# Cross-attention on one core: row sums in one block in a maximum buffer, a third score bank, a step's items in three places per tile, one bias transpose

## What is computed

```python
x = (hidden_states - mu) * jax.lax.rsqrt(var + LN_EPS) * ln_gamma + ln_beta
Q = _split_heads(x @ Wq.T)
K = _split_heads(memory_keys)
V = _split_heads(memory_values)
scores = jnp.einsum('bhsd,bhtd->bhst', Q, K) * scale
scores = jnp.where(mask, scores, -jnp.inf)
probs = jax.nn.softmax(scores, axis=-1)
attn = jnp.einsum('bhst,bhtd->bhsd', probs, V)
return residual + attn.transpose(0, 2, 1, 3).reshape(B, S, HIDDEN) @ Wout.T
```

## Time and profile before

| | us |
|---|---|
| median of 3 runs (734.58 to 739.43) | 737.66 |
| the profiled execution | 736.95 |
| its span, first to last instruction | 735.1 |
| TensorE matmuls busy | 692.0 (94%) |
| VectorE busy | 483.0 (66%) |
| GpSimd busy | 394.1 (54%) |
| ScalarE busy | 351.1 (48%) |

### The profile page before, as it was taken

The page is one execution under the profiler, slowest core; times in us unless marked ns, Lnnn a source line. Parts: engine busy times, 40 slices in busy tenths (PEclk is TensorE's granted clock), DMA queues, the critical chain, the costliest instruction groups (busy, mean ns, idle before and its releaser), DMA issues.

```text
span 735.1 us, 10854 instructions
## 1 busy us (share of the span) xinstructions
PE 692.0 (94%) x3585; PEld 397.1 (54%) x3585; DVE 483.0 (66%) x494; ACT 351.1 (48%) x614; POOL 394.1 (54%) x107
## 2 busy tenths in 40 slices
PE   2789999978999999999999999999999999999998
PEld 2578788534444444444444445444444444478886
DVE  6763432157688878878788887888878776653231
ACT  3741211434566666566666666666666656600000
POOL 1000000047296797967979679796797978930000
PEclk9799999979899999999999999999999999999999
DMA  9621100425426144161441614416244202213231
GB/s 339 180 65 36 44 14 1 119 50 128 100 61 158 38 123 110 51 157 37 122 109 50 157 40 120 111 48 157 49 109 94 84 14 88 86 66 122 98 114 57
DMA packets 39519, 68.10 MB, mean 93 GB/s; under 512 B 5285, under 2 KB 21799, under 8 KB 39471
## 3 DMA queue, kind: packets, MB, share of 16 engines
q1 hardware_dynamic: 39444, 67.64, 33.7%
q10 hardware_dynamic: 36, 0.01, 0.0%
HBM read 25.18 MB, written 4.19 MB: 40 GB/s over the span
## 4 chain that ended last, share of the span: by engine, by line
PE 84%; DVE 6%; SPq 4%; ACT 2%; DMA 2%; issue 2%; POOL 0%; ACTq 0%; DVEq 0%; POOLq 0%
PE SX L914 18%; PE MX L894 17%; PE PV L930 16%; PE MX L1058 12%; PE SM L920 6%; PE PV L857 5%; PE SM L857 4%; DVE mx L715 3%; PE MX L834 2%; SPq L303 1%; SPq L311 1%; DMA PR<-in_x 1%; PE SX L849 1%; PE MX L906 1%; PE MX L900 1%
## 5 line engine op out<-in xcount | busy, mean ns | idle before, releaser
L715 DVE TENSOR_REDUCE mx<-MX 128x1 f32<-128x1024 f32 x256 | 303.2, 1221 | 139.0 <-PE MX L894 138.7
L592 ACT ACTIVATE PR<-SX 128x512 f32<-128x512 f32 x512 | 277.4, 594 | 186.2 <-PE SX L914 186.0
L470 POOL TENSOR_TENSOR acc<-acc,PR 128x2048 f32<-128x2048 f32 x64 | 293.5, 4586 | 31.5 <-ACT PR L592 25.1
L470 POOL TENSOR_TENSOR acc<-PR 128x2048 f32<-128x2048 f32 x16 | 73.3, 4579 | 222.5 <-ACT PR L592 143.3
L914 PE MATMUL SX<-R 99*128 99x512 f32 x512 | 180.7, 432 | 3.2 <-ACT PR L592 2.9
L894 PE MATMUL MX<-R 97*128 97x512 f32 x512 | 165.0, 419 | 15.9 <-DVE mx L715 7.1
L914 PEld LDWEIGHTS SX<-R 99*128 99x128 f32 x512 | 88.7, 190 | 113.8 <-ACT PR L592 93.8
L894 PEld LDWEIGHTS MX<-R 97*128 97x128 f32 x512 | 89.6, 190 | 104.1 <-DVE mx L715 65.0
L930 PE MATMUL PV<-PR,C 128*32 128x512 f32 x1024 | 138.9, 615 | 0.1
L803 DVE TENSOR_TENSOR PR<-PR,MX 128x512 f32<-128x512 f32 x16 | 10.9, 687 | 53.3 <-PE MX L1058 51.8
L1058 PE MATMUL MX<-R 128*128 128x512 f32 x192 | 44.3, 390 | 0.0
(11 more groups left out here) (77 smaller groups left out, 520.3 us busy)
## 6 DMA issues: line engine op xcount, KB each, us to landing
R<-KTh SPq DMA_DIRECT2D x64, 256.0 KB, 4.3
PR<-in_x SPq DMA_DIRECT2D x16, 512.0 KB, 4.1
C<-in_ctx SPq DMA_DIRECT2D x16, 512.0 KB, 3.4
R<-KTl SPq DMA_DIRECT2D x64, 128.0 KB, 3.9
R<-QT SPq DMA_DIRECT2D x64, 128.0 KB, 2.5
acc<-in_L_xattn_Wq SPq DMA_DIRECT2D x8, 512.0 KB, 3.5
R<-QT SPq DMA_DIRECT2D x64, 64.0 KB, 2.1
C<-in_L_xattn_Wout SPq DMA_DIRECT2D x8, 512.0 KB, 3.3
```

What stands on the lines that cost most here:

```text
L470: nc.gpsimd.tensor_tensor(acc[:, :, :], a, PR[:, tt % RING, :, :], ALU.add).then_inc(pool_used, 1)
L592: nc.scalar.activation(PR[:, tt % RING, h, :], SX[h % 2][:, :], ACT.Exp, scale=SCALE).then_inc(exp_done, 1)
L715: nc.vector.tensor_reduce(mx[:, u % 2, c:c + 1], MX[par][:, :], mybir.AxisListType.X, ALU.max, negate=True).then_inc(mx_freed, 1)
```

## The change

- `row_sums`: the direct sums of two tiles and the sum of acc stand in one block of 24 matmuls, an item of slot 1 of the next step, and write into a maximum buffer MX instead of SM. GpSimd adds tiles 0 to 5; tiles 6 and 7 are the direct ones. VectorE turns the sums out of the MX buffer and frees it; the two other parts of the inversion follow the items of slots 2 and 3. After the last step the block stands behind the first two output projections and writes into SX[0].
- SM's bank becomes a third score bank: the scores of a step take the three banks in turn.
- Every slot has three places for items: ahead of the values, behind them, and behind scores 2 and 3; the schedules are written anew.
- The maxima lie in a row (column h * 4 + query tile), the bias is turned by one transpose, and BTh and BTl are 16 x 128 instead of 4 x 512.
- VectorE takes the keys' low part ahead of the query split, and SyncE stacks keys ahead of queries.
- The output projection swaps its two buffers.

```diff
-POOL_TILES = (0, 1, 2, 4, 5, 6)
+BANKS = 3
+PROBS = TT * HPG
+POOL_TILES = (0, 1, 2, 3, 4, 5)
+DIRECT_TILES = (6, 7)
 ADDS = len(POOL_TILES) - 1
-SUM_SLOT = 1
-FIRST_DIRECT = min(set(range(TT)) - set(POOL_TILES))
-SUMS_AT = (2, 5, 7)
-LAST_SUMS_AT = (2, 3, 4)
+SUMS_AT = (2, 3)
...
+def sums(a):
+    return [("sums", a, 0)]
...
 FIRST_STEP = [
-    ([], []),
-    ([], maxima(1, 0, 1)),
-    (maxima(1, 2), maxima(1, 3, 4)),
-    (maxima(1, 5), keys(2) + maxima(1, 6)),
-    (maxima(1, 7), maxima(1, 8, 9)),
-    (maxima(1, 10), maxima(1, 11, 12)),
-    (maxima(1, 13), maxima(1, 14, 15)),
-    (maxima(2, 0), bias(1) + maxima(2, 1, 2, 3)),
+    ([], [], []),
+    ([], maxima(1, 0), maxima(1, 1)),
+    (maxima(1, 2), maxima(1, 3), keys(2)),
+    (maxima(1, 4), maxima(1, 5), maxima(1, 6)),
+    (maxima(1, 7), maxima(1, 8), maxima(1, 9)),
+    (maxima(1, 10), maxima(1, 11), maxima(1, 12)),
+    (maxima(1, 13), maxima(1, 14), maxima(1, 15)),
+    ([], bias(1) + maxima(2, 0), maxima(2, 1, 2, 3)),
 ]
 STEP = [
-    ([], keys(2)),
-    (maxima(1, 4), maxima(1, 5, 6)),
-    ([], maxima(1, 7, 8)),
-    ([], maxima(1, 9, 10)),
-    (maxima(1, 11), maxima(1, 12, 13)),
-    ([], maxima(1, 14, 15)),
-    ([], maxima(2, 0) + bias(1)),
-    (maxima(2, 1), maxima(2, 2, 3)),
+    ([], maxima(1, 4), keys(2)),
+    ([], sums(-1), maxima(1, 5)),
+    ([], maxima(1, 6), maxima(1, 7)),
+    (maxima(1, 8), maxima(1, 9), maxima(1, 10)),
+    ([], maxima(1, 11), maxima(1, 12)),
+    (maxima(1, 13), maxima(1, 14), maxima(1, 15)),
+    ([], bias(1) + maxima(2, 0), maxima(2, 1)),
+    ([], maxima(2, 2), maxima(2, 3)),
 ]
...
     if n == STEPS - 2:
-        items[TT - 1] = (wout(0), wout(1))
+        items[TT - 1] = ([], wout(0), wout(1))
     if n == STEPS - 1:
-        items = [([], []) for _ in range(TT)]
+        items = [([], [], []) for _ in range(TT)]
         for o, tt in zip(range(2, WOUT_BLOCKS), (1, 2, 3, 5, 6, 7)):
-            items[tt] = ([], wout(o))
+            items[tt] = ([], sums(-1) if tt == 1 else [], wout(o))
...
-    BTh = sb("BTh", [HPG, S], F32R)
-    BTl = sb("BTl", [HPG, S], F32R)
-    mx = sb("mx", [P, 2, (ST - 1) * HPG + P], F32)
+    BTh = sb("BTh", [M_ITEMS, P], F32R)
+    BTl = sb("BTl", [M_ITEMS, P], F32R)
+    mx = sb("mx", [P, 2, P], F32)
...
-    SX = [nc.alloc_psum_tensor(f"SX{i}", [P, S], F32) for i in range(2)]
+    SX = [nc.alloc_psum_tensor(f"SX{i}", [P, S], F32) for i in range(BANKS)]
     PV = nc.alloc_psum_tensor("PV", [P, S], F32)
-    SM = nc.alloc_psum_tensor("SM", [P, S], F32)
-    QP = [PV, SM]
+    QP = [PV, SX[2]]
...
-                queries_split(n)
                 keys_split(n)
                 key_rows(u % RING)
+                queries_split(n)
                 query_rows(u % RING)
...
-                nc.scalar.activation(BTh[:, :], MX[par][0:HPG, 0:S], ACT.Copy).then_inc(bt_hi, 1)
+                nc.scalar.activation(BTh[:, :], MX[par][0:M_ITEMS, 0:P], ACT.Copy).then_inc(bt_hi, 1)
...
-            def exps(n, u, tt, pair):
-                    nc.scalar.activation(PR[:, tt % RING, h, :], SX[h % 2][:, :], ACT.Exp, scale=SCALE).then_inc(exp_done, 1)
-            act.sem_inc(exp_done, 2)
+            def exp(n, tt, h):
+                nc.scalar.activation(PR[:, tt % RING, h, :], SX[(HPG * tt + h) % BANKS][:, :], ACT.Exp, scale=SCALE).then_inc(exp_done, 1)
...
-                nc.vector.tensor_reduce(mx[:, u % 2, c:c + 1], MX[par][:, :], mybir.AxisListType.X, ALU.max,
+                nc.vector.tensor_reduce(mx[:, u % 2, i:i + 1], MX[par][:, :], mybir.AxisListType.X, ALU.max,
...
-                    nc.vector.transpose(rsum[:, :], SM[:, :]).then_inc(sums_turned, 1)
+                    nc.vector.transpose(rsum[:, :], bank).then_inc(sums_turned, 1)
...
                         if kind == "keys":
-                            if a == 2:
-                                split_queries(n + a)
                             key_low(n + a, at % 2)
+                            split_queries(n + a)
+                        if kind == "sums":
+                            invert_sums(n + a, 0, MX[at % 2][:, 0:S])
+                            dve.wait_ge(sums_turned, n + a + 1)
+                            dve.sem_inc(mx_freed, 1)
                         at += 1
+                    if tt in SUMS_AT and not first:
+                        invert_sums(n - 1, 1 + SUMS_AT.index(tt))
...
-            step(n, n % RING, items_of(n), LAST_PARITY, LAST_SUMS_AT)
+            step(n, n % RING, items_of(n), LAST_PARITY)
...
             for part in range(3):
-                invert_sums(STEPS - 1, part)
+                invert_sums(STEPS - 1, part, SX[0][:, :])
...
             def bias_item(n, u, par):
-                for st in range(ST):
-                    ins = nc.tensor.transpose(MX[par][:, st * P:(st + 1) * P], mx[:, u % 2, st * HPG:st * HPG + P], ident[:, :])
-                ins.then_inc(bt_ready, 1)
+                nc.tensor.transpose(MX[par][:, 0:P], mx[:, u % 2, :], ident[:, :]).then_inc(bt_ready, 1)
...
+            def score(n, u, tt, h):
+                at = HPG * tt + h
+                if at == 0:
                     pe.wait_ge(bias_in, 32 * (n + 1))
-                pe.wait_ge(exp_done, q + 1)
-                nc.tensor.matmul(SX[h % 2][:, :], KS[u % RING][0:ROWS, h, tt * P:(tt + 1) * P], QS[u % RING][0:ROWS, h, :],
+                if at >= BANKS:
+                    pe.wait_ge(exp_done, PROBS * n + at - BANKS + 1)
+                elif not is_first(n):
+                    pe.wait_ge(exp_done, PROBS * n - PROBS + max(b for b in range(PROBS) if b % BANKS == at) + 1)
+                elif SX[at] is QP[1]:
+                    pe.wait_ge(q_copied, 2 + BATCH * GROUPS)
+                nc.tensor.matmul(SX[at % BANKS][:, :], KS[u % RING][0:ROWS, h, tt * P:(tt + 1) * P], QS[u % RING][0:ROWS, h, :],
                                  start=True, stop=True).then_inc(scores_ready, 1)
...
-            def direct_sum(n, tt):
-                if tt not in POOL_TILES:
-                    if tt == FIRST_DIRECT:
-                        if not is_first(n):
-                            pe.wait_ge(sums_turned, n)
-                        ins = sum_probs(lambda h: PR[:, tt % RING, h, :], True, False)
-                    else:
-                        ins = sum_probs(lambda h: PR[:, tt % RING, h, :], False, False)
-                    ins.then_inc(tile_used, 1)
-            def last_sum(n):
+            def row_sums(n, bank):
+                for tt in DIRECT_TILES:
+                    sum_probs(bank, lambda h: PR[:, tt % RING, h, :], tt == DIRECT_TILES[0], False).then_inc(tile_used, 1)
                 pe.wait_ge(pool_used, ADDS * n + 2 * ADDS)
-                sum_probs(lambda h: acc[:, h, :], False, True).then_inc(sums_done, 1)
+                sum_probs(bank, lambda h: acc[:, h, :], False, True).then_inc(sums_done, 1)
...
+                for tt, (early, with_01, with_23) in enumerate(items):
+                    score(n, u, tt, 0)
+                    score(n, u, tt, 1)
+                    for item in early:
+                        mx_item(*item)
                     if tt >= 1:
                         values(n, u, tt - 1)
                     elif not first:
                         values(n - 1, u + RING - 1, TT - 1)
                     for item in with_01:
                         mx_item(*item)
-                    scores(n, u, tt, 2)
-                    scores(n, u, tt, 3)
-                    for item in with_23[:1]:
-                        mx_item(*item)
-                    if tt >= 1:
-                        direct_sum(n, tt - 1)
-                    elif not first:
-                        direct_sum(n - 1, TT - 1)
-                    if tt == SUM_SLOT and not first:
-                        last_sum(n - 1)
-                    for item in with_23[1:]:
+                    score(n, u, tt, 2)
+                    score(n, u, tt, 3)
+                    for item in with_23:
                         mx_item(*item)
...
             step(n, n % RING, items_of(n), LAST_PARITY, None, VECTOR_FREED_LAST)
             values(n, n % RING, TT - 1)
-            direct_sum(n, TT - 1)
...
-                        ins = nc.tensor.matmul(MX[q][:, cs], a[q][:, g, :], w[half][:, g, :],
+                        ins = nc.tensor.matmul(MX[1 - q][:, cs], a[q][:, g, :], w[half][:, g, :],
...
             project_out(0, 1)
-            last_sum(STEPS - 1)
+            row_sums(STEPS - 1, SX[0][:, :])
             pe.wait_ge(al_done, 2)
```

More of the change, by code:

```diff
@@ L113, in items_of @@
 def items_of(n):
-    items = [([i for i in with_01 if n + i[1] < STEPS], [i for i in with_23 if n + i[1] < STEPS])
-             for with_01, with_23 in (FIRST_STEP if n == 0 else STEP)]
+    items = [tuple([i for i in part if n + i[1] < STEPS] for part in slot) for slot in (FIRST_STEP if n == 0 else STEP)]
     if n == STEPS - 2:
-        items[TT - 1] = (wout(0), wout(1))
+        items[TT - 1] = ([], wout(0), wout(1))
     if n == STEPS - 1:
```

(65 more changed lines are left out.)

72 lines of the change are left out of this document (34 added, 38 removed).

## The result

The changed kernel takes 726.47 us (median, 725.48 to 727.08) against 737.83 of before: ratio 0.9848, 95% interval 0.9824 to 0.9871. A second measurement beside its variants gave 726.18 against 736.3, ratio 0.9866 (0.9843 to 0.9888). The forecast was 729 (722 to 738). The profiled execution has a span of 724.9 us, 10.2 less than before.

What follows compares the result with a forecast made beforehand. TensorE's own list of instructions was taken to set the time. Gains of 10.0 (steps 1 to 13), 0.6, 0.3 and 0.25 made 11.15, less 2.4 in step 0: 737.66 - 8.75 = 729 us, range 722 to 738.

Steps and rivals of the forecast that it cites:

- The price list of TensorE: TensorE's costs start to start, by neighbour: matmul pair 0.45, 32-column block 1.00, its turns 0.23, block before another block 0.88.
- rival without collision: Step 0: the query subtraction does not meet GpSimd's add, so 2.0 us is gained there: 724.5 us, chance 0.2.
- 721.5: Time if, besides no lock in step 0, the earlier low-clock stretch (6.8 us at half clock, worth up to 3.3) goes.
- the border stall: Slot 0 of each step: score 1 needs the last exponential's bank, so values stall 0.54 us.
- three blocks at 1.23 become 2.76, 1.05 gained: Row sums, slot 1: one merged block costs 2.76 instead of 3.69, values ahead 0.12 less; 1.05 us a step gained.
- the collision in step 0: Step 0: VectorE's query subtraction waits for GpSimd's third add, ending at 18.35 instead of 13.9; next step 2.4 us later.
- The thin slots: Most slots, one item behind scores 2 and 3 where two stood: TensorE stalls 0.12 us in an ordinary slot.
- The rival that ate the gain: Loop slots: the chain from scores to values is 0.1 longer in each, losing 11 us: 737 to 738, chance 0.2.
- The port lock: VectorE two-input operations and GpSimd operations exclude each other for a whole instruction; none expected in the loop, one in step 0.
- the chain of 1.58: In a slot, values may start 1.58 us after scores 2 and 3 are issued: 0.43 + 1.09 + 0.06.
- its sums move behind the first output projection, which saves their turns: Step 15: moved row sums save turns; with ScalarE's 0.4 longer delay set against it, 0.3 us gained.
- The term for `first_attn_high`: Step 15: ScalarE's `first_attn_high` stands about 0.4 us longer in the way.

Runs made afterwards that it cites:

- the bank experiment: The changed kernel, with the sequence of score banks skipping one bank once in a step, at score 2 of slot 1: 722.83 us, ratio 0.9817 against before.
- the experiment without the collision: The changed kernel, with VectorE splitting the queries of step 2 ahead of step 0's first maximum: 716.37 us, ratio 0.9739 against before.
- the parted sums: The changed kernel, with the sum of acc parted from the two direct sums by scores 2 and 3 in slot 1: 731.29 us, ratio 0.9925 against before.
- queries ahead of keys: The changed kernel, with VectorE splitting queries ahead of the keys' low part from step 1 on: 726.7 us, ratio 0.9868 against before.

## Why the prediction was right, and where it was off

**The price list of TensorE** carried the forecast. The merged sums came out at 2.69 for 2.76, the values ahead at 0.88 for 0.88, slot 2 at 3.14 for 3.15, slots 3 and 5 (348.70 to 352.41, 355.55 to 359.25) at 3.71 and 3.70 for 3.62, slot 6 at 3.39 for 3.37. The step was to be 29.55 and is 29.31. Two more terms held: GpSimd's fifth add was over 3.9 into the next step (365.88 to 369.75) for a forecast of 4.1, and the bias transpose took the 0.20 that was assumed (331.62 to 331.82).

The number alone would not have told this forecast from its rival without collision (724.5): 726.47 lies between the two. The subtraction of 4.87 in step 0 does. (That rival's second figure, 721.5, should read 721.2: 724.5 less 3.3.)

**The 0.24 a step.** Slot 0 was put at 4.09 and takes 3.73. Two terms were too large. The keys' transposes were taken at 0.97, the distance to a 32-column block in the earlier trace rows; in front of scores they take 340.31 - 339.52 = 0.79. And the border stall: values behind the first score at 0.91 instead of 1.10. The border costs more than this stall all the same: the first score waits there too, and the bank experiment won 0.44 a step.

**The merge by itself.** The term "three blocks at 1.23 become 2.76, 1.05 gained" is right for TensorE's list in the new order and wrong as a gain of its own: alone it made the kernel before slower by 1.9%, about a third of that by the collision in step 0. A kernel with merged sums and respread items but two banks is slower than before as well, by 3.7%: taking the third bank out of the new schedule costs 37 us. The working summed the whole step, which is why the total held.

**The thin slots.** One item behind scores 2 and 3 was to stall TensorE by 0.12 where it has nothing else. Scores to values are 0.64 for an unstalled 0.56: 0.08. The rival that ate the gain by 0.1 more a slot did not come.

**The port lock.** Foreseen by place and time: in the loop none (0.69 and 0.43 for the two operations), in step 0 a subtraction of 4.87 (counted from the first maximum: 13.2 to 18.35 forecast, 13.5 to 18.4 measured). Step 1 began 3.5 later than before, where 2.4 less 0.25 was forecast. Counted from the first maximum it was 38.5 for a forecast of 36.9, and the half clock behind the idle stretch, which the text named but took as even, is worth 2.0 of it. The price of the lost subtraction, 4.4, measured 4.2. The working took this 4.4 for the price of the whole collision. The cast's wait (2.1) and the clock (2.0) belong to it, and so the gain of the case without collision was put too low: the experiment reached 716.4 where that rival had 724.5 or 721.5. Behind this stands the Trainium skill ("SBUF — State Buffer", on the engine side): whichever operation starts first holds the shared pair for the whole instruction. The trace agrees: the third add's exponentials ended at 163.90, the subtraction could start at 164.44, and it ended behind the add.

**Step 1.** The half-clock stretch of the earlier trace rows is not in the changed kernel: its clock there is 1.00. From its first score to the next bias transpose step 1 took 28.09 before, and a later step 25.62 (340.96 to 366.58); the 2.5 between them fit the low clock (0.51 up to 191.40), and are more than half of the 4.11 in the table's second row. The text took this stretch and the new one in step 0 as even, and in size they were (2.5 and 2.0). But the one did not go because the other came: in the experiment without the collision the clock is 1.00 in both places. What went with the new schedule are TensorE's waits at the end of step 0 (from 178.5 to 185.9 it was busy 4.96 us of 7.40 before). The low-clock stretch in the rival "721.5" was thus not tied to the collision.

**The ends.** In step 14 (the table's fourth row) 0.05 was gained for 0.6. The keys' place is empty there, so scores follow scores with no item between, and the values start 1.57 behind the first of them (574.08 to 575.65). This is the chain of 1.58 that the working had priced, where TensorE's own list takes 1.01. Before, the missing keys made the step 1.4 shorter than the others; now it is 0.45 shorter.

The last part lost 2.8 where 0.3 was to be gained. Failed was "its sums move behind the first output projection, which saves their turns". The block there costs 645.29 - 642.58 = 2.71 where the sum of acc took 0.99, so 1.7 is lost behind the projection. Ahead of it one row-sum block less is left, but scores stand right behind scores in three places, and values start 1.65 to 1.76 behind them (595.69 to 597.34, 602.26 to 604.02, 616.61 to 618.29).

The term for `first_attn_high`, "about 0.4 longer", was right. TensorE waits for ScalarE, which waits for GpSimd's normalisation, in both kernels, and 0.34 longer in the changed one (before, then after):

```profile
633.47 0.99 PE L914 MATMUL SX<-R 99*128 99x512 f32 x2 [1.34 <-ACT PR L592]
```

```profile
621.46 0.78 PE L934 MATMUL SX<-R 99*128 99x512 f32 x1 [1.68 <-ACT PR L606]
```

Behind that wait the clock was low in the changed kernel's trace, where before it stayed at 1.00:

```profile
621.00:625.00 4.00, 3.54 (x15) 2.64 (x19) 1.01 (x1) 2.38 (x6) 4.00 (x2) 0.57 0.00 0
```

This low clock is not in every execution. The second profile of the changed kernel, with the clock at 1.00 there, takes 34.34 to the projection and not 35.87. So of the 2.8 that the last part lost, 1.5 belong to the execution and 1.3 to the change.

The errors cancel in part: the gain was put 3.1 too low in twelve steps and 3.3 in step 1, and too high by 0.6 in the step behind the loop, by 3.1 at the end and by 1.4 in step 0: 1.4 too low in all, 8.8 for 10.2. The step itself was forecast well by its list; that the sum over the ends came out so near was in part luck.

## What to carry to other kernels

Where one engine is busy throughout, price its list start to start, by neighbour, and sum the new order slot by slot; a part's gain taken alone may be negative, since a block removed may have covered another engine's lag. Before an operation of VectorE with two SBUF inputs is moved, lay GpSimd's long operations beside it, in the first round of a loop too, where the two run in another phase. With a ring of banks whose length doesn't divide the work of a step, let the sequence skip where there is slack, so that the border meets the oldest bank.

## What the hardware showed that was not expected

A wait can cost more than its length, but its length alone does not tell whether it will. In step 0 of the changed kernel TensorE did nothing from 163.02 to 170.49; its granted clock fell to half within that time, and it then worked about 4 us at 0.52. All seven traces with this wait of 7.5 us show such a stretch, and the two kernels without it have 1.00 there.

The wait of 1.7 us in the last step is different. It was the same, 1.64 to 1.69 us, in six traces of the changed kernel and its variants. Behind it three ran at half clock for about 3.5 us (the changed kernel, the parted sums, queries ahead of keys) and three stayed at 1.00 (the changed kernel's second profile, the bank skip, the early query split). The changed kernel stands on both sides. What decides it these traces do not show; a comparison of two single traces can be wrong by 1.5 us through this alone.
